# A chain of feed-forward and attention stages on one core: products that nobody reads, in front of five waits of TensorE

## What is computed

```python
x = x + 0.5 * _L0_ffn_ref(_layernorm(x), w12, b12, w3, b3)          # silu(x1) * x2, then w3
x = x +       _L0_attn_ref(_layernorm(x), Wq, bq, ..., gq, gk)      # 32 heads of 128, softmax
x = x + 0.5 * _L0_ffn_ref(_layernorm(x), w12, b12, w3, b3)
x = x + 0.5 * _L1_ffn_ref(_layernorm(x), w_gate, w_up, w_down)      # truncated to 8 bits twice
x = x +       _L1_attn_ref(_layernorm(x), Wq, ..., Wo, M, z)        # elu(q)+1 against a fixed memory
x = x + 0.5 * _L1_ffn_ref(_layernorm(x), w_gate, w_up, w_down)
```

## Time and profile before

| | |
|---|---|
| median of 3 runs | 2349.52 us (2348.84 to 2351.33) |
| the profiled execution | 2351.63 us |
| its span, first to last instruction | 2349.8 us |
| busy share of the span: PE, PEld, DVE, ACT, POOL | 97%, 80%, 68%, 48%, 35% |
| mean granted TensorE clock over the span | 0.988 |
| transfers | 210.99 MB, mean 90 GB/s |

### The profile page before, as it was taken

How to read it: one execution, slowest core, us unless ns; L and a number is a source line. 1 busy time by engine, 2 the same in 40 slices (tenths; PEclk the granted TensorE clock), 3 DMA queues, 4 the chain that set the end, 5 groups by cost and what they waited for, 6 DMA issues and landing times. The chain is left out here.

```text
span 2349.8 us, 34378 instructions
## 1 busy us (share of the span) xinstructions
PE 2280.9 (97%) x11044; PEld 1875.4 (80%) x11044; DVE 1604.8 (68%) x2655; ACT 1136.3 (48%) x1846; POOL 830.5 (35%) x736
## 2 busy tenths in 40 slices
PE   7899999999989999999999999999998999898998
PEld 5688888888768888888888888888886788687887
DVE  5644444444368888888888888888886565785665
ACT  3333323322266666666666666666663343352442
POOL 4543332222332122122222222212213466572565
PEclk9999999999999999999999999999999999899999
DMA  3155555555332112212212212211201121031210
GB/s 95 72 176 188 183 174 167 181 174 174 144 108 81 68 53 80 71 49 80 76 45 80 80 54 67 80 59 62 81 23 41 45 73 43 33 121 43 72 59 37
DMA packets 106326, 210.99 MB, mean 90 GB/s; under 512 B 9744, under 2 KB 42512, under 8 KB 102928
## 3 DMA queue, kind: packets, MB, share of 16 engines
q1 hardware_dynamic: 106256, 210.10, 26.4%
HBM read 140.86 MB, written 69.21 MB: 89 GB/s over the span
## 5 line engine op out<-in xcount | busy, mean ns | idle before, releaser
L1064 ACT ACTIVATE at_pT_hi<-ps 128x512 fp32r<-128x512 f32 x512 | 278.1, 595 | 363.7 <-PE ps L1168 363.5
L1106 DVE TENSOR_REDUCE at_small<-ps 128x1 f32<-128x1024 f32 x256 | 312.7, 1222 | 97.9 <-PE ps L356 96.8
L1116 DVE TENSOR_TENSOR at_pT_lo<-ps,at_pT_hi 128x512 fp32r<-128x512 f32 x512 | 327.0, 680 | 2.5 <-ACT at_pT_hi L1064 2.5
L1071 ACT ACTIVATE at_probs<-ps,at_small,rms 128x1024 f32<-128x1024 f32 x256 | 309.2, 1208 | 27.2 <-DVE at_small L1108 22.3
L821 POOL TENSOR_TENSOR qkv_acc<-qkv_acc,qkv_sq 128x512 f32<-128x512 f32 x128 | 167.0, 1305 | 335.7 <-ACT qkv_sq L710 332.2
L1168 PEld LDWEIGHTS ps<-ident,at_probs 128*128 128x128 f32 x2048 | 238.4, 140 | 39.5 <-issue 4.4
L1168 PE MATMUL ps<-ident,at_probs 128*128 128x128 f32 x2048 | 265.5, 272 | 2.8 <-DVE at_pT_lo L1116 2.8
L356 PE MATMUL ps<-ln_xT_hi,qkv_w_hi 128*128 128x512 f32 x496 | 197.1, 397 | 9.2 <-DVE qkv_res L782 9.2
L356 PE MATMUL ps<-ln_xT_hi,ln_xT_lo 128*128 128x512 f32 x768 | 198.4, 393 | 0.0
L1001 POOL TENSOR_TENSOR at_o_lo<-at_o_raw,at_o_hi 128x512 fp32r<-128x512 f32 x32 | 41.3, 1291 | 444.0 <-ACT at_o_hi L1085 444.0
L1130 DVE SCALAR_TENSOR_TENSOR x<-ps,at_small,x 128x512 f32<-128x512 f32 x256 | 192.0, 750 | 8.0 <-PE ps L356 3.1
(11 more groups left out here) (264 smaller groups left out, 5262.3 us busy)
## 6 DMA issues: line engine op xcount, KB each, us to landing
scratch_q_hi<-qkv_q_hi SPq DMA_DIRECT2D x64, 256.0 KB, 2.0
scratch_q_lo<-qkv_q_lo SPq DMA_DIRECT2D x64, 256.0 KB, 2.3
scratch_k<-qkv_res SPq DMA_DIRECT2D x64, 256.0 KB, 2.6
scratch_v<-qkv_res SPq DMA_DIRECT2D x64, 256.0 KB, 2.3
k_raw<-scratch_k SPq DMA_DIRECT2D x32, 512.0 KB, 3.9
at_v_raw<-scratch_v SPq DMA_DIRECT2D x32, 512.0 KB, 3.3
qkv_w<-in_Wq SPq DMA_DIRECT2D x8, 1024.0 KB, 6.4
qkv_w<-in_Wk SPq DMA_DIRECT2D x8, 1024.0 KB, 5.0
```

The source lines that it names most:

```text
L1064: nc.scalar.activation(pT2[jp][0][:, 4 * b:4 * b + 4, w * P:(w + 1) * P], T_BANKS[:, b * HALF:(b + 1) * HALF].rearrange("p (k n) -> p k n" ...
L1071: nc.scalar.activation(probs[l % 4][:], scores(l)[:], ACT.Exp, bias=nbias[:, l % 4:l % 4 + 1], scale=rq[:, l % NT:l % NT + 1], accum_out=s ...
L1106: nc.vector.reduce_max(maxes[:, l % 4:l % 4 + 1], scores(l)[:], AX.X).then_inc(s_max, 1)
L1116: nc.vector.tensor_tensor(pT2[jp][1][out], T_BANKS[:, b * HALF:(b + 1) * HALF].rearrange("p (k n) -> p k n", k=4), pT2[jp][0][out], ALU.su ...
```

## The change

A helper `keep_clock` issues n products of 512 columns whose result is never read. It is called at five places: in `qkv_block` in front of the wait before unit 4 of the first group (36 products, into bank 7), at the end of TensorE's program of the same block (14, bank 7), and in the first `ffn1_block` before the normalisation's step at k = 8, 10 and 11 (14, 12 and 4 products, bank 1). The second `ffn1_block` has no normalisation behind it and so gets none. The operands are tiles that lie in SBUF at that point (`xT.hi`, `wd_hi`), and the products wait for nothing.

```diff
+def keep_clock(nc, out, operand, n):
+    for _ in range(n):
+        nc.tensor.matmul(out, operand[:, 0:P], operand, start=True, stop=True)
@@ qkv_block, TensorE
                     for u in range(UNITS):
                         if start and u == FIRST * NH:
+                            keep_clock(nc, core.bank(7), xT.hi[:, 0, 0:HALF], 36)
                             pe.wait_ge(w_lo_done, 1)
                         if start and u in (0, NH):
                             continue
...
             groups(pe, body)
+            keep_clock(nc, core.bank(7), xT.hi[:, 0, 0:HALF], 14)
@@ ffn1_block
         LN_LAG = 1
+        IDLE = {NT: 14, NT + 2: 12, NT + 3: 4}
         AFTER = LN_LAG + (ln.STEPS - NT if ln else 0)
...
                     down(k, range(IB - 1 if k < 2 else 0, IB)).then_inc(down_done, 1)
+                if ln and k in IDLE:
+                    keep_clock(nc, core.bank(1), wd_hi[:, 0, :], IDLE[k])
                 if ln and k >= LN_LAG:
                     ln.tensor(pe, k - LN_LAG)
```

## The result

The kernel after took 2347.68 us (median of 20 runs, 2344.08 to 2353.83) against 2350.80 for the kernel before (20 runs beside them, 2347.7 to 2356.35). The ratio is 0.9985, with a 95% interval of 0.9978 to 0.9991: 3.5 us less, somewhere between 2.1 and 5.2. The change helps, by less than the 0.2% that I had set as the line, and a microsecond less than forecast. The forecast of 4.5 us lies inside the interval. In absolute terms it was 2345.0 from a median of 2349.52; the kernel before measured 1.3 us more beside the kernel after, and the other 1.4 us of the distance to 2347.68 are what the change brought less than forecast (3.1 by the medians).

A forecast was written before the change was run, and what follows sets the result against it. TensorE, busy 97% of the span, was taken as the bound, its clock halved behind waits. 2.5 + 0 + 2.3 - 0.3 = 4.5 us, from the median of 2349.52 to 2345.0; 8-in-10 range 2342.5 to 2348.2.

The forecast's parts named there:

- Place 1: Projections' wait before unit 4: 36 products hold the clock, 13 products behind take 3.0 instead of 5.6 us; gain 2.5 us.
- Place 2: End of the projections: 14 products speed attention's first scores, but ScalarE waits for `kn` and `k_raw` anyway; gain 0.
- Places 3 to 5: Tail of the first `ffn1_block`: 14, 12 and 4 products keep the clock full; gain 2.3 us, bounds 0 and 2.5.
- the division into 1.8 and 0.5: First `ffn1_block` tail: 1.8 us from VectorE's earlier subtraction for tile 4, 0.5 from tile 7's faster transposition.
- Start of the retrieval: Retrieval's first 12 products end sooner, leaving a 2 us hole where the clock may fall; one in six, 0.3 us off.
- The clock did not fall in the tail: Rival, first `ffn1_block` tail: clock falls all the same between tiles 4 and 5; tail -0.4 us, 2347.4 us; 17%.
- the two rows: Profile stretches from 667.4 (clock stayed) and 1787.0 (clock fell), read against and for transpositions not holding the clock.
- The start of attention: Rival at place 2: `k_raw` sooner or `kn` not pacing, so faster scores gain 1.3 us more; 2343.7 us; 14%.
- place 1 was not caught: Rival: VectorE's first result of K comes late and takes up to all of the 2.5 us; 2347.2 us; 7%.
- the products do hold the clock: Opposed rival: products don't hold the clock and are in the way at place 1 and tail; +4.4, 2353.9 us; 5%.
- point of decision: Place 1: the slower rival comes true once more than six of the 36 products run at half clock.

The follow-up runs named there:

- tail14: Kernel after with only the 14 products at k = 8 in the first `ffn1_block` left; that block took 174.39 us.
- p345_only: Kernel after with only the products in the tail of the first `ffn1_block` left (14, 12, 4); 2348.62 us, ratio 0.9992 to before.
- rt_fill: Kernel after plus 14 and 8 unread products in front of two waits at the end of `retrieval_block`; 2345.69 us, ratio 0.9976 to before.
- rt_fill_kraw: Kernel after plus 14 and 8 unread products in `retrieval_block` and the earlier load of `k_raw`; 2343.24 us, ratio 0.9962 to before.
- all_kraw: Kernel after plus the second head's `k_raw` load moved into the end of the projections; 2345.79 us, ratio 0.9978 to before.
- fill52: Kernel after with 52 instead of 36 products at place 1 and none elsewhere; second group of the projections reached after 73.19 us.
- before_again: The kernel before, unchanged, built and profiled anew; 2349.07 us.
- p1_only: Kernel after with only the 36 products of place 1 left; 2348.31 us, ratio 0.9993 to before.
- tp_fill: Kernel after with 74 fp32 transpositions instead of the 36 products at place 1, nothing elsewhere; second group reached after 70.75 us.
- fill20: Kernel after with 20 instead of 36 products at place 1 and none elsewhere; second group of the projections reached after 72.32 us.
- p2_only: Kernel after with only the 14 products of place 2 left; 2350.83 us, ratio 1.0005 to before.

## Why the prediction came out as it did

*Place 1, 2.5 us: the mechanism held, the size was probably too large.* The products lie in the wait (1.17 us to spare, 1.1 forecast), the clock stays, and VectorE's first result of K does not catch the work: it came at 136.67 in after, ended at 137.41, and unit 12, which needs that bank, began at 137.84, behind no wait: 0.4 us of room, 0.2 forecast. Within the two profiles the term was right (73.36 to 71.01 is 2.35). But it was priced from the one execution in which 13 products were slow. In six executions the second group was reached between 72.08 and 73.66 us, and the mean against the five with 36 products is 73.02 - 71.16 = 1.9 us; timed alone it brought 1.95. With spreads like these the mean is good to some 0.7 us, and four of the six lie within 0.3 us of before, so 2.5 is not excluded. The forecast's bounds were 1.5 to 2.6; I took the end that my profile showed.

*Place 2, nothing: right, with its reason.* The boundary stayed at 2.93 us, the wait for `kn` grew from 0.87 to 1.98 (2.2 forecast, 0.16 less because the transfer came sooner), and the gain of 1.26 us appeared as soon as `k_raw` came early. Eight executions without products at place 2 and without the early load have a mean of 1142.2 us in attention, three with them and without that load 1142.1.

*Places 3 to 5, 2.3 us: the mechanism held, and this is the term that was clearly too large.* The chain over ScalarE's root of tile 6 and VectorE's subtraction came out as worked out (15.23 us from tile 3 to tile 7, 15.3 forecast; tile 7 at 0.63), and against the profile of before tail14 confirms the division into 1.8 and 0.5. In the pair of profiles the block lost 2.36. But eight executions without these products took 175.05 to 176.40 us, 175.49 in the mean, and five with them 173.91 to 174.00, 173.94 in the mean: 1.55 us, good to some 0.5. The 1.8 us for the products ahead belongs to executions in which the clock was down for 6.8 us there; in five of the eight it was down for 3.4, and the same step was worth 0.65 us.

*Start of the retrieval, -0.3:* the hole of 2 us is there. Of the five executions with all products of the tail, the clock fell within some 7 us of the block's start in three (p345_only, rt_fill, rt_fill_kraw), not in after and all_kraw. So it fell more often than the one in six of the forecast, and it cost less than the 1.7 us: in the first two the fall lay over the 12 products, in front of the wait for `rt_r`, and the second unit came 5.20 and 5.01 us after the first, against 4.99. In rt_fill_kraw it lay behind that unit, and the block took 0.45 us more than in rt_fill.

*The sum.* 1.9 + 0.1 + 1.55 is 3.5 us from the stages, and 3.5 by the ratio. That the two agree so well is in part luck, since the last stretch of the projections and the retrieval block, which differ by more than a microsecond between executions, are left out of the first. What was mis-sized is the same in two terms: the slow stretch behind a wait was taken at the length that it had in the profiled execution. In the tail it was near its longest there, at place 1 in its upper half. The forecast took its sum from the median and not from the profiled time, but left the terms as they were.

*The rivals.* The clock did not fall in the tail in any of the five executions with all its products: the holes are there in after (1.62 us of idleness at tile 5), with the clock at 1.00 from 2023 to 2054. The forecast had read the stretch before 1790.3 as speaking for this rival, because of its transpositions. TensorE's time there was mostly products (four of 512 columns, five transpositions), and the stretch with more transpositions, at 667.4, kept its clock, so the two rows never spoke for it. The start of attention did not count, place 1 was not caught, and the products do hold the clock. fill52 shows what "in the way" costs: a stretch that runs 2.4 us past the release costs 2 us, the whole gain. The clock held in it, so the forecast's point of decision, six products at half clock, was not tried.

*What stays open.* The last stretch of the projections, from `sums` on, took 29.9 to 30.1 us in six executions (before, before_again, p1_only, p345_only, tp_fill, fill20), 28.3 to 28.8 in seven, and 26.84 in rt_fill. It goes with the clock: near 630 us it was down for 6.8 us in the six, for 3.4 in the seven and not at all in rt_fill. All four executions of the whole change and its extensions are among the shorter, and four of the other ten. In `retrieval_block`, after and all_kraw took 138.1 and 138.2 us, the ten without the whole change 138.1 to 141.5, 139.6 in the mean. The mean clock rose by 0.0053 with the whole change and by 0.0038 with its parts one by one. Whether these are chance or a benefit of the changed timing cannot be told from so few executions. The 0.4% in the speed of the projections' products is open too.

## What to carry to other kernels

Idleness of TensorE costs twice, by itself and by the slow work behind it; unread products in front of the wait take away the second part if they end just before the release, so they are worth it where something late waits for that work, and a profile must say who. Too few leave the fall to come with the work, too many are paid in full. A gain that depends on when the clock falls should be priced from several executions of the same kernel, stage by stage: here one pair of profiles showed 7.5 us for a change worth 3.5.

## What the runs showed of the hardware

- The same instructions run with the clock down at other places: in `retrieval_block`, without added products there, executions took 138.1 to 141.5 us; the same kernel took 138.13 and 138.78 us there (before, before_again) and 526.9 and 524.1 us up to `sums`.
- At the same wait the clock fell 4.4 us after TensorE went idle in before, 2.3 us after it in before_again (108.25 to 110.58), 5.3 us in p2_only, and 4.5 us in fill20 after its products. Where in a wait it falls could not be read from another execution.
- 74 fp32 transpositions through `ident` went by with the clock at 1.00 for 8.24 us, in a wait in which it fell whenever TensorE was idle (tp_fill).
- From the second group on, the projections' products ran at 0.2324 (5 executions) or 0.2333 us each (9), at the same granted clock of 1.00, with no cause found.
